# Attention layers of a two-layer transformer block: the order in which one DMA-issuing engine works, and the place of a reciprocal

## Chip, cores and metric

One core of one Trainium2 chip. The metric is device time in microseconds of one execution, lower is better; the kernel's time is the median of three runs.

## What is computed

```python
x = L0_attn_x                                # (8, 512, 256) float32
x = layernorm(x + attn(x))                   # 16 heads of 16, biases, head mask, no causal mask
x = layernorm(x + ffn(x))
# ffn: h = x + causal_attention(rmsnorm(x, g1))          rotary q and k, 16 heads of 16
#      y = h + moe(rmsnorm(h, g2))                       8 experts, top 2 of 8, silu(x wg) * (x wu) @ wd
```

Every attention ends in softmax(scores) @ v. The kernel computes the sum of exponentials (the denominator) beside the weighted sum, so the output of a group of heads has to be divided by its denominators before the output projection.

## The kernel before

The program has three stages: the two attention layers in one stage (`attention_layers`), the routing of tokens to experts, and the expert tiles with the final normalisation. The change lies in the first alone.

**Units, halves, groups.** A unit u is one of the 8 sequences in one of the 2 layers: u 0 to 7 is the first layer ("plain"), 8 to 15 the second ("causal"). A unit has two halves h of 8 heads, a half has two groups of 4 heads; n counts groups from 0 to 63, u is n // 4 and g is n % 4. Every engine runs the same outer loop, one step for each n, and each step has four quarters. In step n TensorE makes the scores of group n (L778, diagonal blocks masked by L839), ScalarE takes their exponentials (L1067), TensorE weighs v with them (L879), and, three groups ahead, TensorE makes the scores from which VectorE takes row maxima (L783, L1171). In between each step does pieces of other units: projections, rotary embedding, the output projection, the residual, statistics.

**The path of a half's output.** ScalarE empties the output of group n - 1 into `a_o` in quarter 2 of step n (L1074). SyncE, which issues every DMA of this stage in one fixed order, stores it in DRAM (`store_o`, L299). When both groups of a half are stored, `load_o` reads back the denominators alone as a 128x32 tile `a_den` (L308) and the outputs without them, `a_o_half` (L312). VectorE inverts `a_den` in place (`invert`, L1259). SyncE stores the inverse (`store_inv`, L317) and reads it back spread over the 16 dimensions of each head, `a_inv_half` (`load_inv`, L325). GpSimd multiplies (`normalise`, L474) and splits the result into high and low halves in float16, `a_aT` (L478, L480). TensorE takes `a_aT` in the output projection (`project_out`, L705), in steps with g = 2, quarters 2 and 3, and VectorE adds the residual (L1301 for the first layer, L1306 for the second).

**What GpSimd does around it.** In an odd step of the second layer GpSimd splits q and k (L455, L460, after VectorE's rotary sum L1271), then calls `normalise`, then in steps with g = 3 adds the residual (L527), then splits a piece of expert weights (L539, L541). In the following even step with g = 2 it makes the low half of the layer's output (`part_low`, L532), for which VectorE's L1306 waits.

**What SyncE does around it.** Its other DMAs are the q and k tiles (L255, L260, L275), the row maxima (`load_rows`, L283, after ScalarE's L1010), the next input (`load_x`, L240 or L245), the residual (`load_res`, L334), stores of results (`store_x`, L343, `store_part`, L352), and in steps 0 to 47 and the one after the pieces of expert weights that are split in the background (`store_weights` L372, `load_weights` L364). A wait on SyncE holds back everything behind it.

The lines that a sentence can't say, of `load_o`:

```python
for i in range(2):
    sync.wait_ge(o_stored[i], 16 * (h + 1))
...
sync.dma_start(den[:, h % 2], heads[:, DH].rearrange("k (c e) -> k c e", e=32)
               ).then_inc(den_loaded[h % 2], 16)
```

## Time and profile before

| | us |
|---|---|
| median of 3 runs | 1419.68 (1417.67 to 1426.33) |
| the profiled execution | 1423.02 |
| its span | 1421.3 |
| TensorE (PE) busy | 1259.9, 89% of the span |
| VectorE (DVE) busy | 959.2, 67% |
| ScalarE (ACT) busy | 823.6, 58% |
| GpSimd (POOL) busy | 778.3, 55% |
| mean granted clock of TensorE | 0.945 of full speed |

The times of one execution are read from its start. The attention stage lasts until about 880 us, the routing until about 930, the expert tiles and the final normalisation to the end. An engine's idle time is put down to what it waited for last.

### The profile page before, as it was taken

Reading aid. Unit: us, or ns where it says so; the run is one execution under the profiler, and the core shown is the slowest. Engines: PE = TensorE matmul, PEld = TensorE weight load, DVE = VectorE, ACT = ScalarE, POOL = GpSimd, SP = SyncE. Lnnn points to the kernel's source line nnn. Section 1 sums busy time; section 2 is a strip of 40 time slices with the busy share of each in tenths; the row PEclk is TensorE's granted clock in tenths of the full one; section 3 lists DMA queues with packets and bytes.
Section 4 is the critical chain, followed back from the end, with each engine's and each line's share of the span. In section 5 each row is a group of like instructions: output and inputs, shape, how many; then the busy total and the mean of one; then the engine's idle time right before and its main releaser. Section 6 shows DMA issues by size and latency. Waiting matters only on the chain. (4 is left out here: it accounts for less than half of the span.)

```text
span 1421.3 us, 33080 instructions
## 1 busy us (share of the span) xinstructions
PE 1259.9 (89%) x11471; PEld 693.0 (49%) x11472; DVE 959.2 (67%) x1776; ACT 823.6 (58%) x1676; POOL 778.3 (55%) x820
## 2 busy tenths in 40 slices
PE   3999999999999999999999995379999999999980
PEld 1222222322223444444444443358888888888860
DVE  7788888888897886978888736924444444444434
ACT  4078788788888776766676663134343434344434
POOL 5044465556546667576645333056666666666643
PEclk7589999999999999999999897689999999999996
DMA  6336676767767878687766433875222222223226
GB/s 183 66 78 175 184 183 188 193 186 204 199 184 215 227 220 226 206 217 200 209 165 164 115 123 126 226 210 121 42 47 42 47 44 45 42 44 48 38 27 240
DMA packets 157657, 202.53 MB, mean 143 GB/s; under 512 B 30760, under 2 KB 120616, under 8 KB 157544
## 3 DMA queue, kind: packets, MB, share of 16 engines
q1 hardware_dynamic: 140968, 181.60, 46.6%
q0 software_dynamic: 16576, 19.45, 8.6%
q8 instruction: 68, 1.11, 0.3%
q14 instruction: 45, 0.37, 0.1%
HBM read 110.40 MB, written 81.81 MB: 135 GB/s over the span
## 5 line engine op out<-in xcount | busy, mean ns | idle before, releaser
L1067 ACT ACTIVATE a_probs<-a_ps_s 128x512 f32<-128x512 f32 (+2 forms) x896 | 460.4, 569 | 165.1 <-PE a_ps_s L778 160.1
L1171 DVE TENSOR_REDUCE a_shift_max<-a_ps_m 128x1 f16<-128x512 f32 x512 | 320.7, 684 | 54.7 <-PE a_ps_m L783 53.4
L783 PE MATMUL a_ps_m<-a_qkx 48*128 48x128 f16 (+3 forms) x1408 | 285.2, 303 | 20.2 <-DVE a_shift_max L1171 8.7
L1868 PE MATMUL e_ps_gu<-e_xT,w_up 128*128 128x256 f16 (+1 forms) x2574 | 290.0, 269 | 4.5 <-issue 3.0
L778 PE MATMUL a_ps_s<-a_qkx 49*128 49x128 f16 (+3 forms) x1408 | 276.0, 296 | 14.3 <-ACT a_probs L1067 14.3
L1868 PEld LDWEIGHTS e_ps_gu<-e_xT,w_up 128*128 x2574 | 242.2, 98 | 38.6 <-issue 8.7
L879 PE MATMUL a_ps_o<-a_probs,a_v_one 128*32 128x512 f32 (+3 forms) x2048 | 233.8, 529 | 2.6 <-ACT a_o L1074 2.6
L778 PEld LDWEIGHTS a_ps_s<-a_qkx 49*128 49x128 f16 x1408 | 90.1, 95 | 265.4 <-ACT a_probs L1067 151.6
L1804 POOL DMA_INDIRECT h<-e_y,e_put x74 | 118.7, 1604 | 88.6 <-DVE e_y L1968 57.6
L474 POOL TENSOR_TENSOR a_o_half<-a_o_half,a_inv_half 128x512 f32<-128x512 f32 x31 | 40.0, 1289 | 222.2 <-DMA a_inv_half<-a_inv_dram 222.2
L1981 DVE TENSOR_TENSOR e_h<-e_gate,e_ps_gu 128x512 f32<-128x512 f32 (+4 forms) x156 | 79.5, 530 | 120.8 <-ACT e_gate L1931 90.2
L1931 ACT ACTIVATE e_gate<-e_ps_gu 128x512 f32<-128x512 f32 (+1 forms) x78 | 44.9, 575 | 196.5 <-PE e_ps_gu L1868 160.6
L1890 PE MATMUL e_ps_y<-w_down,e_h 128*128 x1258 | 146.2, 273 | 11.2 <-issue 9.8
L1171 DVE TENSOR_REDUCE a_neg_off<-a_ps_m 128x1 f32<-128x384 f32 (+2 forms) x256 | 138.6, 545 | 10.6 <-PE a_ps_m L783 9.7
L1988 DVE TENSOR_TENSOR e_h<-e_h 128x512 f16<-128x512 f32 (+4 forms) x156 | 84.3, 540 | 85.2 <-ACT e_h L1936 43.6
L1890 PEld LDWEIGHTS e_ps_y<-w_down,e_h 128*128 128x128 f16 x1258 | 114.7, 97 | 41.3 <-issue 21.4
L455 POOL CAST a_qk<-a_q 128x1024 f16<-128x1024 f32 x32 | 33.2, 1037 | 157.3 <-DVE a_q L1271 91.9
L1171 DVE TENSOR_REDUCE a_neg_max<-a_ps_m 128x4 f32<-128x512 f32 x128 | 87.9, 687 | 42.4 <-PE a_ps_m L783 41.7
L783 PEld LDWEIGHTS a_ps_m<-a_qkx 48*128 48x128 f16 x1408 | 84.7, 95 | 63.2 <-DVE a_shift_max L1171 37.6
L654 PE MATMUL a_ps_x<-a_xT,w_proj 128*128 128x512 f16 x384 | 100.9, 402 | 14.9 <-DVE w_proj L1360 11.0
L1816 POOL DMA_INDIRECT e_share<-weights,e_find x74 | 76.6, 1035 | 42.3 <-issue 42.3
L1790 POOL DMA_INDIRECT e_x<-part,e_take x74 | 74.2, 1003 | 40.5 <-issue 39.1
(240 smaller groups left out, 1673.7 us busy)
## 6 DMA issues: line engine op xcount, KB each, us to landing
a_qkx<-a_qk_dram SPq DMA_DIRECT2D x192, 128.0 KB, 4.3
a_qk_dram<-a_qk SPq DMA_DIRECT2D x32, 512.0 KB
a_o_dram<-a_o SPq DMA_DIRECT2D x62, 256.0 KB, 2.9
part<-a_part SPq DMA_DIRECT2D x16, 512.0 KB, 5.6
a_q_swap<-a_q SPq DMA_DIRECT2D x64, 128.0 KB
a_o_half<-a_o_dram SPq DMA_DIRECT2D x31, 256.0 KB
a_inv_half<-a_inv_dram SPq DMA_DIRECT2D x31, 256.0 KB
spare<-in_wg SPq DMA_DIRECT2D x16, 352.0 KB, 5.6
```

The costliest lines, as they stand in the source:

```text
L654: mm = pe.matmul(ps_x[:], t.w_proj[:, 4 * layer + w, wh, k, m * P:(m + 1) * P], xT[:, u % 2, xh, k, :], start=n == 0, stop=n == 5)
L778: return pe.matmul(out, kx[first:first + 49, r, pair, kt * P:(kt + 1) * P], qx[first:first + 49, r, pair, q0:q1], start=start, stop=stop)
L783: return pe.matmul(out, qx[first:first + 48, r, pair, q * P:(q + 1) * P], kx[first:first + 48, r, pair, k0:k1], start=start, stop=stop)
L879: mm = pe.matmul(ps_o[32 * j:32 * (j + 1), S - w:S], v_one[:, u % 2, kt, g * HG + j, :], probs[:, kt // 2, j, first:first + w], start=kt = ...
L1067: act.activation(dst, src, ACT.Exp).then_inc(exp_out, 1)
L1171: vector.tensor_reduce(out, src, AX.X, ALU.max, negate=True).then_inc(max_out, 1)
L1804: pool.indirect_dma_start(t.h_dram, bass.IndirectOffsetOnAxis(ap=put[:, s, half:half + 1], axis=0), y[:, s, half], None, compute_op=ALU.ad ...
L1816: pool.indirect_dma_start(share[:, s, half:half + 1], None, t.weight_dram, bass.IndirectOffsetOnAxis(ap=find[:, s, half:half + 1], axis=0) ...
L1868: mm = pe.matmul(ps_gu[:, bank, kind, f % 2, 0:width(r, s)], w[:, ds(e, 1)].rearrange("p o f -> p (o f)"), xT[:, s, xh, k, 0:width(r, s)], ...
L1890: mm = pe.matmul(ps_y[:, s, half], h[:, s, hh, f, half * P:(half + 1) * P], w[:, ds(e, 1)].rearrange("p o f -> p (o f)"), start=c == 0, st ...
L1981: op = vector.tensor_tensor(h32[0:rows, bank, m, 0:w], gate[0:rows, bank, m, 0:w], ps_gu[0:rows, bank, 1, m, 0:w], ALU.mult)
L1988: op = vector.tensor_tensor(low, h32[0:rows, bank, m, 0:w], h[0:rows, s, 0, f, 0:w], ALU.subtract)
```

## The change

`after` does the same instructions and the same DMAs with the same waits. Two things stand in another order.

```diff
                 if n % 2 == 0:
                     swap((n + 6) // 2)
                     load_qk((n + 4) // 2)
+                    store_o(n - 1)
+                    load_o(n // 2 - 1)
                     if g == 0:
                         store_part(u - 3)
                         load_res(u - 1)
                     elif u + 3 > 0:
                         load_x(u + 3)
-                    store_o(n - 1)
                     for m in weights_at(n - 1):
                         store_weights(m)
                         load_weights(m + 2)
-                    load_o(n // 2 - 1)
                 else:
+                    store_inv((n - 3) // 2)
                     load_rows((n + 1) // 2)
+                    load_inv((n - 3) // 2)
                     load_last(n - 1)
                     load_last(n)
-                    store_inv((n - 3) // 2)
                     store_o(n - 1)
                     if g == 3:
                         store_x(u - 2)
-                    load_inv((n - 3) // 2)
...
                         if quarter < 2:
                             rope_sum((n + 5) // 2, quarter)
-                        if quarter == 1:
+                        if quarter == 0:
                             invert((n - 3) // 2)
```

SyncE, steps 40 and 41 (second layer, h = 19). `a_o` is a group's output, `part` and `a_x_res` the layer's result and the residual, `w_down` and `spare` the expert weights. Before:

```order
L352 DMA part<-a_part 128x4x512
L334 DMA a_x_res<-x 128x4x256
L299 DMA a_o_dram<-a_o 128x512
L372 DMA w_down_hi<-a_w_part 128x704
L372 DMA w_down_lo<-a_w_part 128x704
L364 DMA spare<-in_wd 128x704
L308 DMA a_den<-a_o_dram 128x1x32
L312 DMA a_o_half<-a_o_dram 128x1x512
L283 DMA a_qkx<-a_rows 1x4x512 x2
L317 DMA a_inv_dram<-a_den 128x32
L299 DMA a_o_dram<-a_o 128x512
L325 DMA a_inv_half<-a_inv_dram 128x1x512
```

The same place of SyncE in the changed kernel:

```order
L299 DMA a_o_dram<-a_o 128x512
L308 DMA a_den<-a_o_dram 128x1x32
L312 DMA a_o_half<-a_o_dram 128x1x512
L352 DMA part<-a_part 128x4x512
L334 DMA a_x_res<-x 128x4x256
L372 DMA w_down_hi<-a_w_part 128x704
L372 DMA w_down_lo<-a_w_part 128x704
L364 DMA spare<-in_wd 128x704
L317 DMA a_inv_dram<-a_den 128x32
L283 DMA a_qkx<-a_rows 1x4x512 x2
L325 DMA a_inv_half<-a_inv_dram 128x1x512
L299 DMA a_o_dram<-a_o 128x512
```

The store of the output and the two loads that wait for it moved ahead of the result, the residual and the three weight DMAs; the store of the inverse moved ahead of the rows, and its load ahead of the next store of an output.

VectorE in step 41, before. `a_neg_off` and `a_neg_max` are row maxima of a later group, `a_q` the rotary sum:

```order
L1271 TENSOR_TENSOR a_q<-a_q_cos,a_q_swap 128x512
L1171 TENSOR_REDUCE a_neg_off<-a_ps_m 128x2
L1171 TENSOR_REDUCE a_neg_max<-a_ps_m 128x2x2
L1171 TENSOR_REDUCE a_neg_off<-a_ps_m 128x1
L1326 SCALAR_TENSOR_TENSOR a_hid<-a_hid,a_rms,g 128x256
L1271 TENSOR_TENSOR a_q<-a_q_cos,a_q_swap 128x512
L1259 RECIPROCAL a_den<-a_den 128x32
```

and in the changed kernel:

```order
L1271 TENSOR_TENSOR a_q<-a_q_cos,a_q_swap 128x512
L1259 RECIPROCAL a_den<-a_den 128x32
L1171 TENSOR_REDUCE a_neg_off<-a_ps_m 128x2
L1171 TENSOR_REDUCE a_neg_max<-a_ps_m 128x2x2
L1171 TENSOR_REDUCE a_neg_off<-a_ps_m 128x1
L1326 SCALAR_TENSOR_TENSOR a_hid<-a_hid,a_rms,g 128x256
L1271 TENSOR_TENSOR a_q<-a_q_cos,a_q_swap 128x512
```

The reciprocal moved ahead of one quarter's three maxima, one scaling and the second rotary sum.

## Rows read from the trace of the kernel before

**Rows 1.** Windows: time, busy us by engine (instructions), granted clock, DMA share, GB/s.

```profile
303.53:354.12 50.59, 47.50 (x339) 14.50 (x337) 44.68 (x81) 42.79 (x85) 28.71 (x30) 1.00 0.72 194
509.30:556.35 47.05, 44.59 (x512) 19.99 (x511) 39.56 (x76) 33.17 (x70) 29.78 (x30) 1.00 0.80 225
556.35:607.80 51.45, 47.48 (x514) 20.96 (x515) 43.38 (x72) 32.87 (x74) 32.73 (x27) 0.93 0.76 218
607.80:658.03 50.23, 46.60 (x557) 21.67 (x556) 40.49 (x70) 32.80 (x72) 33.83 (x27) 1.00 0.81 218
658.03:707.87 49.84, 47.10 (x550) 21.47 (x547) 39.06 (x69) 32.70 (x73) 29.88 (x24) 0.97 0.72 192
707.87:755.31 47.44, 46.02 (x555) 21.57 (x556) 39.46 (x71) 32.70 (x72) 26.46 (x20) 1.00 0.70 176
...
802.49:855.71 53.22, 49.61 (x570) 22.43 (x567) 23.38 (x46) 35.67 (x83) 12.10 (x11) 0.96 0.37 111
```

**Rows 2.** Waits of GpSimd and VectorE: us in total, times, longest us.

```profile
POOL a_o_half L474 <- DMA a_inv_half<-a_inv_dram: 222.2, 31, 20.9
...
DVE a_hid L1306 <- POOL a_part L532: 15.7, 4, 6.5
...
DVE a_den L1259 <- DMA a_den<-a_o_dram: 1.5, 2, 0.9
```

**Rows 3.** Timeline around 600 us, VectorE and GpSimd: start us, us, instruction, idle before.

```profile
593.32 2.01 DVE L1271 TENSOR_TENSOR a_q<-a_q_cos,a_q_swap 128x512 f32<-128x512 f32 x1
...
597.90 0.34 DVE L1259 RECIPROCAL a_den<-a_den 128x32 f32<-128x32 f32 x1
...
599.16 2.13 POOL L460 TENSOR_TENSOR a_qk<-a_q,a_qk 128x1024 f16<-128x1024 f32 x1
603.95 1.27 POOL L474 TENSOR_TENSOR a_o_half<-a_o_half,a_inv_half 128x512 f32<-128x512 f32 x1 [2.66 <-DMA a_inv_half<-a_inv_dram]
...
612.48 0.69 DVE L1306 TENSOR_TENSOR a_hid<-a_ps_x,a_x_res 128x512 f32<-128x512 f32 x1 [4.11 <-POOL a_part L532]
```

**Rows 4.** Timeline of TensorE at 558 us.

```profile
557.93 2.71 PE L705 MATMUL a_ps_x<-w_proj,a_aT 128*128 128x256 f16 x12 [2.53 <-POOL a_aT L480]
```

**Rows 5.** Timeline of SyncE around the same inversion: its DMA issues.

```profile
586.17 0.38 SPq L352 DMA_DIRECT2D part<-a_part  x1
586.65 0.45 SPq L334 DMA_DIRECT2D a_x_res<-x  x1
587.15 1.04 SPq L299 DMA_DIRECT2D a_o_dram<-a_o  x1
...
589.68 0.43 SPq L364 DMA_DIRECT2D spare<-in_wd  x1
593.58 0.65 SPq L308 DMA_DIRECT2D a_den<-a_o_dram  x1
594.28 0.63 SPq L312 DMA_DIRECT2D a_o_half<-a_o_dram  x1
594.96 1.29 SPq L283 DMA_DIRECT2D a_qkx<-a_rows  x2
598.27 0.32 SPq L317 DMA_DIRECT2D a_inv_dram<-a_den  x1
...
599.68 0.64 SPq L325 DMA_DIRECT2D a_inv_half<-a_inv_dram  x1
```

**Rows 6.** Windows in that stretch, same columns as the first group.

```profile
589.50:592.50 3.00, 2.87 (x36) 0.93 (x29) 2.94 (x6) 2.02 (x5) 3.00 (x4) 1.00 1.08 375
```

**Rows 7.** DMA issues 598 to 601 us: KB each, median us to landing.

```profile
a_inv_dram<-a_den SPq DMA_DIRECT2D x1, 16.0 KB, 1.4
```

**Rows 8.** Timeline of SyncE and GpSimd near the end of the stage.

```profile
825.36 0.33 SPq L299 DMA_DIRECT2D a_o_dram<-a_o  x1
...
827.40 0.62 SPq L308 DMA_DIRECT2D a_den<-a_o_dram  x1
...
832.20 1.28 SPq L283 DMA_DIRECT2D a_qkx<-a_rows  x2
...
835.06 0.64 SPq L325 DMA_DIRECT2D a_inv_half<-a_inv_dram  x1
839.01 1.27 POOL L474 TENSOR_TENSOR a_o_half<-a_o_half,a_inv_half 128x512 f32<-128x512 f32 x1 [8.97 <-DMA a_inv_half<-a_inv_dram]
```

## The prediction

> **What bounds the kernel now.** I read the busy shares by engine first, then the table of waits, then windows of one unit each, and last the timeline at the places where the windows are too long. TensorE is busy for 89% of the span, but the change touches only the attention stage, and only its waits, so the question is which wait there ends last. The table of waits has a large candidate: GpSimd idles 222.2 us in 31 pieces for the inverse that comes back from DRAM [rows 2]. That is no gain in itself, since GpSimd is not the engine that sets the pace. What counts is who waits behind it.
>
> In the first layer nobody does. A unit there takes 50.59 us with TensorE 47.5, VectorE 44.7 and ScalarE 42.8 busy, and GpSimd 28.7 [rows 1]: GpSimd's idle time is cover. In the second layer a unit that starts at the normalisation before its output projection takes 47.05 us where nothing stalls, but the next three take 51.45, 50.23 and 49.84, and then one takes 47.44 [rows 1]. At the start of the first long one TensorE waits 2.53 us for `a_aT`, and its 12 matmuls then take 2.71 us [rows 4]; the window has a granted clock of 0.93 [rows 1]. At the start of the second VectorE waits 4.11 us for GpSimd's `part_low` [rows 3], one of four such waits of 15.7 us, the longest 6.5 [rows 2]. GpSimd reaches `part_low` late because `normalise` ahead of it sat 2.66 us for the inverse [rows 3]. So the second layer has a chain: store of the output, denominators back, reciprocal, store of the inverse, inverse back, `normalise`, `part_low`, residual. It ends last once in a unit, and this is the chain that the change shortens.
>
> **The change, step by step, for the half inverted at 597.9 us.** *Denominators.* Before, the output store is issued at 587.15 and the denominators, which wait for it, at 593.58: 6.43 us [rows 5]. The same pair with nothing ahead takes 2.04 us (825.36 to 827.40) [rows 8]. The gain is therefore at most 4.4 us plus the 0.98 us of issue ahead of the store (586.17 to 587.15), and at least that 0.98. Ahead of the store stand the q and k loads, which stay there, and two transfers of 512 KB, which go behind. At the rate of the stretch, 375 GB/s [rows 6], these two take 1.05 MB / 375 = 2.8 us, nearer to the bytes than to either end. I take the denominators 2.7 us sooner: issued at 590.9.
>
> *Behind them.* SyncE still has to issue the output's load, the result, the residual and three weight DMAs. Before, the stretch from 586.17 to the end of the last weight issue at 590.11 plus the output's load of 0.63 comes to 4.57, less the output's store of 1.04: 3.5 us. SyncE is free at 590.9 + 0.65 + 3.5 = 595.0.
>
> *Reciprocal.* It now follows the first rotary sum, which ends at 593.32 + 2.01 = 595.3, and takes 0.34 [rows 3]: done at 595.7 and not 598.2. The denominators have to be there by 595.3; the nearest small transfer, 16 KB, lands in 1.4 us [rows 7], so they are there at 592.3, and the cover is 3.0 us. Even at their old time (593.58 + 1.4 = 595.0) VectorE would not wait. The maxima behind the reciprocal start 0.34 us later and those behind its old place as before: nothing.
>
> *Store and load of the inverse.* SyncE issues the store at 595.8. Here the new order has its price: the output's load, result, residual and weights, 1984 KB or 2.03 MB that before had mostly drained, have been issued in the 4 us ahead of it. At 375 GB/s [rows 6] they need 5.4 us from 591.0, to 596.4, and the store lands at 595.8 + 1.4 = 597.2 as if alone. In the meantime SyncE issues the rows for 1.29 us [rows 5], to 597.4, so the inverse's load goes out at 597.4 and not at 599.68: 2.3 us. The load itself took 603.95 - 599.68 = 4.27 us [rows 3, 5] behind an output store and takes 3.95 at the quietest place [rows 8], so another 0.2 comes from that. The inverse arrives 2.5 us sooner. GpSimd sat idle 2.66 us there, from the end of its split of q and k at 601.29 [rows 3], so almost all of it is used; the next to end last is that split.
>
> The rate decides this step. 375 GB/s is a stretch with large transfers alone; over a whole unit, with the small descriptors of q and k in it, the rate is 218 to 225 [rows 1]. At 218 the 2.03 MB last 9.3 us, to 600.3, and the inverse's store, if it has to let them pass, would land at some 601.2 and its load go out 1.5 us later than now. I take 375, since what stands in this backlog is what ran at that rate, and keep the other end for a rival.
>
> That a small store pays for what was issued ahead of it is the rule of the Trainium skill that speaks against this change. The page "DMA: Bandwidth & Descriptors" says, in "Queues, rings and completion order", that each DMA engine takes descriptors in ring order and that a semaphore's increment lands only after every earlier write of that engine. Without the rule the store would land in 1.4 us at any rate, each stall would give 2.5 us whatever the backlog, and the rival below would fall away. The output store bears the rule out: 6.43 us behind other transfers against 2.04 alone [rows 5, 8].
>
> **The sum.** I apply 2.5 us to each unit's stall.
>
> - Unit at 556: TensorE's wait of 2.53 us goes, and the excess over a unit without a stall is 51.45 - 47.05 = 4.4 us, of which the rest is half-speed matmuls behind the wait (the clock of 0.93). I take 3.9, since the clock may fall for another reason.
> - Unit at 608: 2.5 of 4.11 us of wait, on an excess of 3.18: 1.9.
> - Unit at 658: the four waits of VectorE sum to 15.7, less 6.5 and 4.11 leaves 5.1 for two, this being the larger with some 3.3. 2.5 of 3.3, on an excess of 2.79: 2.1.
> - Unit at 708: excess 0.39, all of it: 0.4.
> - End of the stage (unit at 802, VectorE's wait of 6.5 us): no weights are moved there, and the output store has nothing ahead, so the denominators gain nothing. The inverse's load follows the rows, issued at 832.20 for 1.28 us, at 833.5 and not at 835.06 [rows 8]: 1.5 us sooner.
> - First layer: the same sooner inverse shortens GpSimd's idle time and nobody's wait: 0. The transfers that now start 3 to 4 us later (next input, residual, result, weight pieces) are needed a step, 12 us, later or more; at nothing, with that step as cover. If the residual came late, GpSimd's idle time for the inverse would still stand behind it.
>
> Together 3.9 + 1.9 + 2.1 + 0.4 + 1.5 = 9.8 us. The profiled execution took 1423.02 us (span 1421.3), 3.3 above the median of 1419.68; against its own time the sum gives 1413.2, and carried to the median 1409.9. I say **1410 us**.
>
> **Rivals.** *The backlog cancels it* (no change). The inverse's load goes out when it did before if the backlog ends at about 598.7, 7.7 us from 591.0, a rate of 264 GB/s; that is between the two rates above. For it: the unit's mean is under that. Against: the stretch itself was at 375, and halves in steps with g = 2 have 512 KB less ahead. Then only the 1.5 us at the end, where no weights are moved, are left: 1418.
>
> *More than the stalls goes* (faster). GpSimd idles a few us before each normalisation of the second layer; with these gone, q and k are stored sooner too and no stretch falls to half clock. All four excesses (10.8 us) and the 6.5 us at the end: 17.3 us, 1402.
>
> *The backlog delays the inverse* (slower). The same mechanism beyond that point: weights, result and residual are issued as one block directly ahead of the inverse's store, and at 218 GB/s they hold it until 601.2. The inverse is then 1.5 us later than before at each of the eight normalisations of the second layer that stand ahead of an output projection, the unit without a stall included: 8 x 1.5 = 12 us, 1432. It decides from 264 GB/s down. The rows of maxima, issued right behind the store, would be late with it and could only add to this.
>
> *The change doesn't do what it says*: excluded by the listed order, which has the moves on both engines.
>
> **Chances.** Forecast (5 to 14 us faster) 0.52; no change (within 5 either way) 0.24; more than 14 faster 0.14; slower by more than 5, 0.10. Some 1%, 14 us, is what a measurement of this kernel can tell from no change. So faster by over 1% 0.15, within 1% 0.77 (part of the slower case lies within), slower by over 1% 0.08. The range takes in the forecast, the case without gain, and the nearer part of the faster one: 1401 to 1422.
>
> **What the changed profile should show.** GpSimd's idle time for the inverse well below 222 us, near 130; 31 halves with an output store and denominators 3 to 5 us apart; VectorE's reciprocal directly after the first rotary sum with at most 2 us of waiting in all; the wait of VectorE for `part_low` down from 15.7 to some 7 us; units of the second layer at 47 to 48.5 us; units of the first layer unchanged at 50.6. I am wrong if VectorE's wait at L1259 is over 10 us, if the inverse's store takes over 4 us to land, or if the first layer's units change.

## The result and the profile after

The changed kernel takes 1466.46 us (median of 4 runs, 1465.73 to 1468.12), the kernel before 1418.68 in the same comparison (1417.25 to 1426.33): 1.033 times as long, with a 95% interval from 1.031 to 1.035. That is 47.8 us more, where 9.8 less were forecast.

The busy times, from the page of the changed kernel's profile:

```profile
span 1464.2 us, 33080 instructions
PE 1285.2 (88%) x11471; PEld 699.3 (48%) x11472; DVE 963.0 (66%) x1776; ACT 827.1 (56%) x1676; POOL 774.8 (53%) x820
```

VectorE, ScalarE and GpSimd are as busy as before, within 4 us. TensorE is busy for 25 us more with the same instructions: its mean granted clock was 0.936, after 0.945. The waits of the whole run (us in total, times, longest us), against [rows 2]:

```profile
POOL a_o_half L474 <- DMA a_inv_half<-a_inv_dram: 207.5, 31, 17.4
...
PEld a_ps_m L783 <- DMA a_qkx<-a_qk_dram: 33.9, 16, 5.7
...
POOL a_x_res L489 <- DMA a_x_res<-in_x: 31.0, 6, 8.6
...
PE a_ps_m L783 <- DMA a_qkx<-a_qk_dram: 29.5, 16, 5.5
```

GpSimd's idle time for the inverse, which I wanted at 130 us, only fell from 222.2 to 207.5. Two waits stand out that were small or absent before: TensorE waits for the q and k tiles of the maxima (in the attention stage, from 100 to 900 us, 3.1 us before and 27.0 now), and GpSimd for the residual, 31.0 us, all in the first layer. TensorE's wait for `a_aT`, which the forecast set out to remove at one place, hardly moved: 5.9 us before, 5.3 now. VectorE's wait for the denominators is gone, and its wait for `part_low` is down from 15.7 to 3.3 us; so two of the signs that I named came true while the time went the other way. Of the three signs of being wrong, two came: the inverse's store took over 4 us to land, and the first layer's units changed.

The engine that was moved says more. The waits of SyncE, the changed kernel:

```profile
SPq L307 <- DMA a_o_dram<-a_o: 133.3, 29, 6.3
SPq L275 <- DMA a_qk_dram<-a_qk: 84.7, 31, 5.9
SPq L325 <- DMA a_inv_dram<-a_den: 82.7, 29, 4.8
SPq L283 <- ACT a_rows L1010: 62.0, 20, 22.9
SPq L317 <- DVE a_den L1259: 20.4, 12, 5.7
```

and of the kernel before:

```profile
SPq L307 <- DMA a_o_dram<-a_o: 120.0, 29, 6.8
SPq L283 <- ACT a_rows L1010: 114.9, 26, 24.7
SPq L275 <- DMA a_qk_dram<-a_qk: 85.7, 31, 7.4
...
SPq L325 <- DMA a_inv_dram<-a_den: 15.3, 18, 2.1
```

SyncE stands 67.4 us longer for the inverse to land in DRAM and 13.3 us longer for the output. What went down is its wait for ScalarE (L283), 52.9 us: time in which SyncE was ahead of the engines. That was its slack, and the change spent it.

Windows of four units of the second layer as one, then of seven units of the first (columns as in [rows 1]). Before:

```profile
499.28:695.91 196.63, 183.69 (x2101) 83.11 (x2101) 158.66 (x279) 132.13 (x287) 129.53 (x106) 0.97 0.78 217
139.56:499.28 359.72, 340.01 (x2532) 109.32 (x2529) 311.24 (x559) 297.22 (x583) 207.63 (x204) 1.00 0.72 195
```

and after:

```profile
518.67:737.32 218.65, 197.60 (x2106) 86.67 (x2105) 156.90 (x280) 134.47 (x288) 129.05 (x106) 0.90 0.73 195
138.04:518.67 380.63, 347.32 (x2524) 109.99 (x2522) 315.57 (x560) 298.41 (x582) 209.83 (x205) 0.98 0.70 184
```

Here a unit runs from ScalarE's emptying of the output of its first group (L1074) to the next unit's. The second layer's four units lost 22.0 us: 13.9 in which TensorE was busy longer (the clock fell from 0.97 to 0.90) and 8.1 in which it stood idle. The first layer's seven lost 20.9: 7.3 busy and 13.6 idle. The DMA engines have the same bytes to move and are busy for a smaller share, 0.73 after 0.78. Over a whole unit the loss is not a lack of bandwidth; DMAs are issued later. In the last units, which have no weights to move, the time is 137.4 before and 138.8 after.

The same half as in [rows 3, 5, 7] (h = 19), SyncE in the changed kernel:

```profile
618.74 0.42 SPq L299 DMA_DIRECT2D a_o_dram<-a_o  x1
624.10 0.65 SPq L308 DMA_DIRECT2D a_den<-a_o_dram  x1
...
628.42 0.49 SPq L364 DMA_DIRECT2D spare<-in_wd  x1
628.95 0.51 SPq L317 DMA_DIRECT2D a_inv_dram<-a_den  x1
629.50 1.29 SPq L283 DMA_DIRECT2D a_qkx<-a_rows  x2
635.64 0.63 SPq L325 DMA_DIRECT2D a_inv_half<-a_inv_dram  x1
...
638.28 0.74 SPq L260 DMA_DIRECT2D a_qk_dram<-a_qk  x1
639.12 3.52 SPq L255 DMA_DIRECT2D a_q_swap<-a_q  x4
643.72 2.85 SPq L275 DMA_DIRECT2D a_qkx<-a_qk_dram  x6
646.61 0.42 SPq L299 DMA_DIRECT2D a_o_dram<-a_o  x1
```

Read two gaps. From the output's store to the denominators SyncE stands still for 4.9 us with nothing behind it issued. From the rows to the inverse's load it stands again, 4.85 us (630.79 to 635.64): the store of 16 KB took 6.7 us to land. Before, the first pair was 6.43 us apart, but with three weight DMAs issued in between [rows 5], and the second landing took 1.4 us [rows 7]. Over the stretch from 500 to 800 us the median time of the inverse's store from issue to landing went from 1.4 us to

```profile
a_inv_dram<-a_den SPq DMA_DIRECT2D x11, 16.0 KB, 5.0
```

GpSimd ended the split of q and k at 635.27, and its store goes out at 638.28. One even output store to the next is 27.9 us (618.74 to 646.61); before it was 23.5 (587.15 to 610.66). SyncE's own round is longer by 4.4 us. Some 0.5 of that is that the result and the residual fall into this round now and the next input into the other; the rest is its two waits.

Why the store was late is seen in the landing times of one block, from 512.4 to 523 us of the changed kernel (KB each, median us from issue to landing):

```profile
part<-a_part SPq DMA_DIRECT2D x1, 512.0 KB, 5.6
a_x_res<-in_x SPq DMA_DIRECT2D x1, 512.0 KB, 7.4
spare<-in_wd SPq DMA_DIRECT2D x1, 352.0 KB, 6.7
...
a_inv_dram<-a_den SPq DMA_DIRECT2D x1, 16.0 KB, 6.3
```

and in the windows of that stretch:

```profile
511.00:513.00 2.00, 1.95 (x17) 0.81 (x17) 0.69 (x1) 0.49 (x1) 1.30 (x1) 0.55 0.01 2
513.00:516.00 3.00, 3.00 (x23) 1.06 (x21) 2.56 (x5) 2.64 (x6) 0.00 (x0) 0.50 0.62 133
516.00:519.00 3.00, 3.00 (x29) 1.18 (x26) 2.02 (x4) 2.48 (x6) 0.20 (x1) 0.50 1.03 340
```

While SyncE waits for the output to land the DMA engines run dry (share 0.01, 2 GB/s); then the block of 1984 KB (output's load, result, residual, weights) starts from nothing, and the small store behind it lands with it. The Trainium skill says on the page "DMA: Bandwidth & Descriptors", in "Queues, rings and completion order", that a semaphore's increment lands only after every earlier write of the same DMA engine; it is the rule that the prediction weighed. The trace agrees: the last piece of the block, issued at 516.12, landed 6.7 us later, at 522.8, and the store, issued at 516.64, 6.3 us later, at 522.9.

How SyncE's lateness reaches the q and k tiles is seen one half earlier, where h = 18 is inverted, in the changed kernel:

```profile
605.56 0.63 SPq L325 DMA_DIRECT2D a_inv_half<-a_inv_dram  x1
...
610.39 0.46 SPq L260 DMA_DIRECT2D a_qk_dram<-a_qk  x1
...
616.03 2.66 SPq L275 DMA_DIRECT2D a_qkx<-a_qk_dram  x6
```

GpSimd's split of q and k had ended at 605.05. SyncE stood until 605.56 for the inverse, then had five issues to make up, and stored q and k only at 610.39, 5.3 us after they were ready; before the change, at the same place, it was 1.0 us (split ended at 576.55, store at 577.51). The loads that depend on that store go out at 616.03, and TensorE's timeline shows the wait for such loads:

```profile
511.05 0.50 PE L783 MATMUL a_ps_m<-a_qkx 48*128 48x256 f16 x2 [2.28 <-DMA a_qkx<-a_qk_dram]
...
623.77 0.60 PE L783 MATMUL a_ps_m<-a_qkx 48*128 48x256 f16 x2 [5.47 <-DMA a_qkx<-a_qk_dram]
```

with windows around the second:

```profile
610.00:616.00 6.00, 6.00 (x76) 3.44 (x75) 5.43 (x10) 3.77 (x8) 5.86 (x5) 1.00 1.01 328
616.00:620.00 4.00, 2.31 (x26) 0.77 (x24) 1.35 (x3) 1.69 (x3) 3.84 (x5) 1.00 0.82 142
620.00:624.00 4.00, 0.23 (x2) 0.16 (x3) 0.00 (x0) 0.00 (x0) 3.92 (x4) 0.55 0.81 131
624.00:626.00 2.00, 2.00 (x17) 0.70 (x15) 0.81 (x2) 0.64 (x2) 0.18 (x1) 0.50 0.05 8
```

TensorE stands for 5.47 us and afterwards works at 0.50 of full speed, its 1.2 GHz level. So a wait is followed by a second price, longer matmuls.

### The profile page after: what moved, and what is told of

It reads as the page before. It is cut to its first block and busy times, and to the rows that moved or that the text cites. A ratio compares the mean times of both kernels' runs of the same rounds, so it can differ in the third digit from the quotient of the medians.

```text
span 1464.2 us, 33080 instructions
## 1 busy us (share of the span) xinstructions
PE 1285.2 (88%) x11471; PEld 699.3 (48%) x11472; DVE 963.0 (66%) x1776; ACT 827.1 (56%) x1676; POOL 774.8 (53%) x820
## 5 line engine op out<-in xcount | busy, mean ns | idle before, releaser
L1067 ACT ACTIVATE a_probs<-a_ps_s 128x512 f32<-128x512 f32 (+2 forms) x896 | 462.4, 569 | 204.0 <-PE a_ps_s L778 198.9
L783 PE MATMUL a_ps_m<-a_qkx 48*128 48x128 f16 (+3 forms) x1408 | 291.9, 309 | 44.4 <-DMA a_qkx<-a_qk_dram 29.5
L778 PE MATMUL a_ps_s<-a_qkx 49*128 49x128 f16 (+3 forms) x1408 | 284.9, 304 | 13.5 <-ACT a_probs L1067 13.0
L879 PE MATMUL a_ps_o<-a_probs,a_v_one 128*32 128x512 f32 (+3 forms) x2048 | 237.5, 537 | 2.6 <-ACT a_o L1074 2.6
L1171 DVE TENSOR_REDUCE a_neg_off<-a_ps_m 128x1 f32<-128x384 f32 (+2 forms) x256 | 138.7, 545 | 26.8 <-PE a_ps_m L783 26.0
L474 POOL TENSOR_TENSOR a_o_half<-a_o_half,a_inv_half 128x512 f32<-128x512 f32 x31 | 39.5, 1274 | 207.5 <-DMA a_inv_half<-a_inv_dram 207.5
L654 PE MATMUL a_ps_x<-a_xT,w_proj 128*128 128x512 f16 x384 | 108.0, 423 | 13.6 <-DVE w_proj L1360 10.9
L1816 POOL DMA_INDIRECT e_share<-weights,e_find x74 | 76.0, 1027 | 42.3 <-issue 42.3
L1790 POOL DMA_INDIRECT e_x<-part,e_take x74 | 72.0, 973 | 40.2 <-issue 40.2
```

Source lines behind the costliest of these rows:

```text
L654: mm = pe.matmul(ps_x[:], t.w_proj[:, 4 * layer + w, wh, k, m * P:(m + 1) * P], xT[:, u % 2, xh, k, :], start=n == 0, stop=n == 5)
L778: return pe.matmul(out, kx[first:first + 49, r, pair, kt * P:(kt + 1) * P], qx[first:first + 49, r, pair, q0:q1], start=start, stop=stop)
L783: return pe.matmul(out, qx[first:first + 48, r, pair, q * P:(q + 1) * P], kx[first:first + 48, r, pair, k0:k1], start=start, stop=stop)
L879: mm = pe.matmul(ps_o[32 * j:32 * (j + 1), S - w:S], v_one[:, u % 2, kt, g * HG + j, :], probs[:, kt // 2, j, first:first + w], start=kt = ...
L1067: act.activation(dst, src, ACT.Exp).then_inc(exp_out, 1)
L1171: vector.tensor_reduce(out, src, AX.X, ALU.max, negate=True).then_inc(max_out, 1)
```

## The experiments

The theory after the result: SyncE is near its limit, and time in which it stands still for a landing is the loss. The rivals: it is the backlog's delay of the inverse alone (the rival of the prediction, larger than priced); or VectorE or GpSimd wait at a new place. The experiments first take the change apart, then move single pieces. "Before" as baseline of a diff is the kernel before, "changed" the kernel after. Differences in us are taken from 1418.68 and 1466.46, the medians above. The ratios are each run's own comparison with the kernel before, which had 1416.95 to 1418.89 there; so a difference in us is good to some 2 us.

**The half of the change in even steps.** From before:

```diff
                     load_qk((n + 4) // 2)
+                    store_o(n - 1)
+                    load_o(n // 2 - 1)
...
-                    store_o(n - 1)
...
-                    load_o(n // 2 - 1)
```

> Only the even steps are changed: store of the output, denominators and output load ahead of result or input, residual and weight pieces; odd steps and VectorE as before. Theory 1 (the block of 1.5 to 2 MB now stands directly ahead of the inverse's store, which lands 5 us after its issue instead of 1.7, and SyncE stands still meanwhile, so the q and k tiles come late): most of the loss is here, 1440 to 1465 us, and SyncE's wait at L325 is 50 us or more, not 15. Theory 2 (the reciprocal ahead of the row maxima holds VectorE): nothing or a gain here, 1410 to 1420.

Measured: 1440.09 us, 1.016 times before (1.012 to 1.020). Nearly half of the loss comes from this alone. SyncE's wait for the inverse's landing rises from 15.3 to 46.7 us although its store and load stand where they stood: the block of transfers now starts late and is in front of them. The waits of TensorE say what that costs: for `a_aT` 20.0 us in the attention stage, after 5.9, and for q and k only 4.7. That is the late inverse of the prediction's slower rival, by itself.

**The half in odd steps, with the reciprocal.** From before:

```diff
+                    store_inv((n - 3) // 2)
                     load_rows((n + 1) // 2)
+                    load_inv((n - 3) // 2)
...
-                    store_inv((n - 3) // 2)
...
-                    load_inv((n - 3) // 2)
...
-                        if quarter == 1:
+                        if quarter == 0:
```

> Only the odd steps and VectorE are changed: store of the inverse ahead of the rows, its load right behind them, reciprocal a quarter sooner; even steps as before. Theory 1: no block ahead of the inverse's store, so no loss, 1408 to 1421 us, with SyncE's wait at L325 under 25 us and GpSimd's wait for the inverse under 200. Theory 2: the whole loss, 1450 to 1470, with VectorE waiting over 10 us at L1259.

Measured: 1432.49 us, 1.013 (1.009 to 1.016). VectorE waits 16.1 us for the denominators and SyncE 61.8 us for the reciprocal. The two halves alone lose 21.4 and 13.8 us, together 35.2 of 47.8; what is left only appears when both are there.

**The reciprocal alone.** From before:

```diff
-                        if quarter == 1:
+                        if quarter == 0:
```

> Only the reciprocal moves, a quarter sooner on VectorE; SyncE's order is as before. Theory 1: 1415 to 1421 us, no difference. Theory 2: the denominators, which come as late as before, hold up the maxima: 1435 or more.

Measured: 1436.6 us, 1.013 (1.009 to 1.017). The waits of VectorE:

```profile
DVE a_den L1259 <- DMA a_den<-a_o_dram: 19.5, 15, 2.7
```

The loss of 17.9 us is nearly all in the first layer (374.6 us for its seven units after 359.7), while the second layer's four units are even 2.2 us shorter (194.4). The waits are not: 9.6 of the 19.5 us fall before 500 us, 9.9 after. So a wait of VectorE costs in the first layer, where it is next to the pace, with 44.7 of 50.59 us busy [rows 1]. The reciprocal early in the second layer alone was not tried. In the changed kernel this wait is nought, since the denominators come earlier.

**The change without the reciprocal's move.** From changed:

```diff
-                        if quarter == 0:
+                        if quarter == 1:
```

> The whole change of SyncE's order, the reciprocal as before. Since VectorE waits 0.0 us for denominators in the changed kernel, Theory 1 (SyncE's two uncovered waits in a cycle of two steps) gives no less than the change itself, 1460 to 1480 us: the inverse's store now waits for a later reciprocal and the rows stand behind it. If the quarter is part of the loss in combination too, under 1455.

Measured: 1474.6 us, 1.041 (1.038 to 1.043). Inside the full change the reciprocal's move is a gain of 8.1 us (1.041 against 1.033); VectorE is not where the loss lies.

**The inverse's load back at its place.** From changed:

```diff
                     load_rows((n + 1) // 2)
-                    load_inv((n - 3) // 2)
...
                         store_x(u - 2)
+                    load_inv((n - 3) // 2)
```

> The whole change, but the load of the inverse stands again behind the next output store and the store of x. Theory 1: the two issues ahead of the wait hide only 0.5 to 1 us of 5, so it stays slow, 1450 to 1466 us. Theory 1b (the block alone is harmless, it is the early load of the inverse that holds the output store and all behind it): most of the loss goes, under 1430.

Measured: 1433.16 us, 1.012 (1.008 to 1.015). One line gives back 33.3 of 47.8 us. SyncE's wait at that load falls from 82.7 to 37.3 us, as other issues lie between the store and its load again, TensorE's for the q and k tiles from 27.0 to 2.1, and the first layer is back at 361.0 us. This is the largest single step. GpSimd still waits 13.8 us for the residual here, so a wait of that size costs the first layer next to nothing. In the second layer's four units 9.1 us of the loss stay, with 14.9 us of TensorE's waiting for `a_aT`: the late inverse again.

**The inverse's load alone moved forward.** From before:

```diff
                     load_rows((n + 1) // 2)
+                    store_inv((n - 3) // 2)
+                    load_inv((n - 3) // 2)
...
-                    store_inv((n - 3) // 2)
...
-                    load_inv((n - 3) // 2)
```

> Only the load of the inverse moves, ahead of the output's store in odd steps; the bulk transfers and VectorE stay. Theory 1': with nothing large ahead of the inverse's store it lands in 1.5 us and the uncovered wait is small: 1415 to 1424 us, TensorE's wait for q and k under 6 us. If the early load costs by itself whatever is ahead, 1430 or more.

Measured: 1436.33 us, 1.012 (1.009 to 1.015), with 40.6 us of SyncE's waiting for the inverse to land and 12.4 us of TensorE's for q and k. The inverse's store, which moves with it, lands as before here (1.77 us from the store to its load over 31 halves, 1.70 before). The early load costs 17.7 us even without the block behind an idle stretch.

**Only the output's store ahead.** From before:

```diff
                     load_qk((n + 4) // 2)
+                    store_o(n - 1)
...
-                    store_o(n - 1)
```

> Only one thing is moved in the kernel before: in even steps the output's store goes ahead of result, residual or input; the loads that wait for it stay behind the weight pieces, and odd steps and VectorE are as before. Theory A (every load that waits for its store is harmless as long as the bulk transfers stand between them, the loss is SyncE standing still with idle DMA engines): the denominators are issued 2 us sooner, SyncE's wait at L307 falls, and the time is 1410 to 1420 us. Theory B (result, residual and input must go out first, whatever SyncE waits for): 1425 or more, with GpSimd waiting for the residual at L489.

Measured: 1412.87 us, 0.997 (0.995 to 0.999): a gain of 0.3%, small but clear of none by its interval. The waits of SyncE:

```profile
SPq L283 <- ACT a_rows L1010: 161.2, 32, 24.6
SPq L275 <- DMA a_qk_dram<-a_qk: 82.1, 30, 6.4
SPq L307 <- DMA a_o_dram<-a_o: 66.3, 29, 4.5
```

Here the store is followed by its old neighbours, which are issued while it lands, and the wait for it halves from 120.0 to 66.3 us. The time saved appears as slack for ScalarE's rows, 161.2 after 114.9. It is the one part of the change that moves a DMA forward without a wait for a landing moving with it, and the best version here. Where the gain arises is not settled: in the profiled executions the seven and the four units are within 1 us of before, and the last three units, without weights, take 131.8 us after 137.4.

**The same, with the inverse's store and the reciprocal early.** From the kernel of the last experiment:

```diff
+                    store_inv((n - 3) // 2)
                     load_rows((n + 1) // 2)
...
-                    store_inv((n - 3) // 2)
...
-                        if quarter == 1:
+                        if quarter == 0:
```

> As the run before, and the reciprocal a quarter sooner with the inverse's store ahead of the rows; the inverse's load stays where it was. If VectorE's 19.5 us at L1259 came only from denominators 2 us too late, they fall under 5 us and the time is 1405 to 1418. If they stay over 10 us, 1425 to 1435.

Measured: 1423.79 us, 1.005 (1.003 to 1.007). VectorE waits 11.9 us for denominators that left only 1 to 2 us sooner, and SyncE 114.1 us at the inverse's store. Here too the first layer loses (371.0 us) and the second layer's four units gain (192.9, the least of all versions).

**The same as the best, the inverse's load ahead of the result.** From that kernel:

```diff
+                    load_inv((n - 3) // 2)
                     if g == 3:
                         store_x(u - 2)
-                    load_inv((n - 3) // 2)
```

> The output's store ahead of result, residual or input in even steps, and in odd steps the load of the inverse ahead of the store of x (512 KB), behind the output's store. Theory 1': the inverse lands about 1 us sooner in steps with g = 3 and nothing else moves: 1409 to 1415 us against 1413 of the store alone. A loss of over 5 us would say that even 0.5 us of uncovered wait counts.

Measured: 1421.64 us, 1.002 (1.000 to 1.005), from 12 runs of 1413.63 to 1430.48. One DMA of cover less, and the gain is gone; TensorE's wait for q and k is 8.2 us.

**Weights of even steps issued in the odd ones.** From changed:

```diff
-                    for m in weights_at(n - 1):
-                        store_weights(m)
-                        load_weights(m + 2)
                 else:
...
-                    for m in weights_at(n - 1):
+                    for m in weights_at(n - 2) + weights_at(n - 1):
```

> The whole change, but the weight pieces of even steps (704 KB) are issued in the odd step behind the load of the inverse and the stores, with that step's own. Theory 1 (the inverse's store lands late behind the block, and SyncE waits for it at L325): that wait falls from 83 us by at least a third, TensorE's wait for q and k tiles with it, and the time is 1430 to 1450. Theory C (the length of SyncE's order is what counts, not the bytes ahead of the inverse): L325 stays over 65 us and the time at 1460 or more.

Measured: 1472.01 us, 1.040 (1.035 to 1.044). With 704 KB less ahead of it SyncE's wait for the inverse's landing fell from 82.7 to 48.7 us, so the backlog does decide the landing. But the kernel got no faster: 45.4 us are now spent waiting for the reciprocal at the inverse's store. If the inverse's delay by the backlog were the whole loss, this would have helped. What the landing gives back is taken at the wait next in line, since the two stand in one issuer. The run has a weakness: the late weights now stand ahead of the store of q and k, and GpSimd's wait for the swapped q rises from 7.1 to 17.1 us, so it does not separate the two theories cleanly.

**q and k stored ahead of the inverse's load.** From changed:

```diff
-                    load_inv((n - 3) // 2)
...
                     store_o(n - 1)
+                    store_qk((n + 5) // 2)
+                    load_inv((n - 3) // 2)
...
-                    store_qk((n + 5) // 2)
```

> The whole change, but in odd steps the output's store and the store of q and k go out ahead of the load of the inverse and its wait. Theory 1' (of the change's 48 us the larger part, some 30, is the wait for the landed inverse standing ahead of the store of q and k, whose load TensorE needs at the start of the second step after): TensorE's wait for q and k tiles falls from 27 us to under 8 and the time to 1425 to 1442, although SyncE still stands still at L325. Theory C (SyncE's total of waits is what counts): over 1455.

Measured: 1459.09 us, 1.029 (1.026 to 1.032). The first layer is back at 360.9 us and the second is as bad as before, 219.8 for its four units. There the store of q and k waits for GpSimd's split (42.3 us at L260 over the run, 5.5 in the changed kernel), and the inverse waits behind it: TensorE now stands 16.7 us for `a_aT`. I had expected both layers to recover. The first layer's loss is the issue of q and k and its surroundings held up by the inverse; the second layer's is not that alone. The last three units lose here too, 149.8 us after 137.4.

**The same store early in the best version.** From that kernel:

```diff
                     store_o(n - 1)
+                    store_qk((n + 5) // 2)
                     if g == 3:
...
-                    store_qk((n + 5) // 2)
```

> The output's store ahead of result, residual or input in even steps, and in odd steps the store of q and k directly behind the output's store, ahead of the store of x, the load of the inverse and the weight pieces. Theory 1': q and k tiles come sooner, where they were late TensorE gains, but the inverse's load waits for GpSimd's split of q and k: between 1405 and 1420 us. Clearly slower, over 1425, if the inverse is the tighter of the two.

Measured: 1479.67 us, 1.044 (1.042 to 1.047). A clear miss, and the slowest kernel of all: SyncE waits for GpSimd at L260 and at the weights' store (34.0 and 23.2 us), the inverse's load stands behind that, and GpSimd, which has to normalise before it splits weights, waits for the inverse. It is again a wait put ahead of work that others need.

**The inverse's load issued by GpSimd.** From changed:

```diff
-                    load_inv((n - 3) // 2)
...
             def normalise(h):
...
+                    pool.wait_ge(inv_stored[s], 16 * (h // 2 + 1))
...
+                    pool.dma_start(inv_half[:, s], src.broadcast_to([8, DH, S])).then_inc(inv_loaded[s], 16)
```

> The whole change, but the load of the inverse is issued by GpSimd, which waits for it anyway, directly ahead of normalise; SyncE no longer waits at L325. All bytes and their order of need stay. Theory S (SyncE standing still is the loss): 83 us of its waits go, and the time falls from 1466 to 1410 to 1435. Theory T (traffic: the inverse lands late behind the bulk transfers whoever issues it): 1455 or more.

Measured: 1475.78 us, 1.042 (1.036 to 1.047). Half of what it was to show came: TensorE's wait for q and k fell from 27.0 to 5.8 us once SyncE no longer waited for the inverse's landing. But GpSimd asks for the inverse only after its own split and then waits for all of it (lines are shifted by 4):

```profile
POOL a_o_half L478 <- DMA a_inv_half<-a_inv_dram: 160.8, 30, 8.3
POOL a_inv_half L475 <- DMA a_inv_dram<-a_den: 76.6, 12, 13.3
PE a_ps_x L709 <- POOL a_aT L484: 33.4, 11, 4.1
```

The hand-over adds a wait of TensorE of its own, 33.4 us after 5.3 in the changed kernel, so that the total says nothing of how much SyncE's wait was worth.

**The same hand-over in the best version.** From that kernel, the same lines.

> The output's store ahead of result, residual or input in even steps as in e5, and the inverse's load issued by GpSimd. Theory S: SyncE waits only 12 us there in e5, so little is to be had: 1405 to 1418. If GpSimd's own issue is dear, 1420 or more.

Measured: 1471.85 us, 1.040 (1.036 to 1.044), 59 us slower than the version that it is made from. SyncE has 194.8 us of slack at L283 and TensorE waits 41.0 us for `a_aT`. Slack on the issuer is worth nothing if the engine that issues instead is on the path.

**The second layer without its weight traffic, changed and before.** The pieces of `w_down` (numbers 32 to 47, counted from 0, all moved in the second layer) are neither loaded nor stored in the stage, so that its content is left out; GpSimd's splits stay, and the stores are made behind the stage. From changed and from before:

```diff
-                if 0 <= m < NW:
+                if 0 <= m < NW and m < KEPT:
```

> The whole change without the loads and stores of the 16 weight pieces of the last matrix during the second layer (left out of the computation: w_down's content; GpSimd still does the splitting, and 32 stores follow at the end of the stage). To be read against e16. Theory S and Theory T both: the 29 us of the second layer shrink, under 10, since SyncE gets 48 issues (some 25 us) of slack back and the DMA engines 704 KB a step less. Were the loss in VectorE's or GpSimd's order, all 29 would stay.

> The kernel before with the same left out (w_down's content), as the measure for e15: 1415 to 1440 us with the stores at the end; the difference of the two is what the change costs with slack given back: 15 us of the first layer, and 0 to 10 of the second.

Measured: 1451.17 us, 1.024 (1.021 to 1.027), and 1421.98, 1.005 (1.003 to 1.006). The changed order is 29.2 us behind, not 47.8. Windows of the same four units of the second layer, the changed order and the order before:

```profile
517.88:714.03 196.15, 183.94 (x2101) 83.65 (x2101) 159.83 (x279) 132.33 (x287) 129.13 (x106) 0.97 0.67 169
```

```profile
496.56:685.07 188.51, 181.94 (x2101) 82.28 (x2101) 158.89 (x279) 131.95 (x288) 129.86 (x106) 0.98 0.68 169
```

A loss of 7.6 us where it was 22.0, and the clock stays at 0.97. Two thirds of the second layer's loss hang on the weight traffic; of the first layer's, where nothing was taken away, 16.2 us stay (and 22.0 in the next pair; so a sum of one profiled execution varies).

**Only the bytes taken away.** The same DMAs are issued, with 32 of 704 columns each (of `w_down` again only that much is moved in the stage, and its content is left out). From changed and from before:

```diff
-                        sync.dma_start(dst, w_part[:, m % 2, hl]).then_inc(w_stored[m % 2], 16)
+                        sync.dma_start(dst[:, 0:cut(m)], w_part[:, m % 2, hl, 0:cut(m)]).then_inc(w_stored[m % 2], 16)
```

> The whole change; the weight DMAs of the last 16 pieces are all issued, but each moves 32 of 704 columns (left out of the computation: w_down's content; 32 full stores follow at the end of the stage). To be read against e18, units 8 to 11. Theory S (SyncE's own time: issues and the waits for landings): the issues are back but the landings of the inverse and output are quicker for lack of bytes, so the loss is above e15's 8 us, 12 to 20, if issue time counts. Theory T (bytes): about 8 us or less, as in e15 against e16.

> The kernel before with the same small weight DMAs (w_down's content left out), the measure for e17: 1418 to 1428 us, as e16; units 8 to 11 at 187 to 192 us.

Measured: 1461.47 us, 1.031 (1.027 to 1.034), and 1425.54, 1.006 (1.004 to 1.008). The four units take 199.4 and 189.2 us:

```profile
519.11:718.47 199.36, 185.08 (x2101) 83.48 (x2101) 153.99 (x279) 132.90 (x287) 128.52 (x106) 0.97 0.68 167
```

```profile
495.63:684.88 189.25, 181.69 (x2101) 82.86 (x2101) 158.81 (x280) 131.71 (x288) 129.99 (x106) 0.98 0.69 171
```

So the loss of 22.0 us is 10.1 with the issues and their waits kept and the bytes gone, and 7.6 with both gone. The 10.1 lies between what the two theories had asked for, nearer to the one in which the bytes count. The split is some 12 us for the bytes of the weights, 2.5 for their issue, and 7.6 for the order of what remains. The first layer, the same in both pairs, came out 5.8 us apart, so the 12 is a size and the 2.5 is not told from nothing. That the bytes act by way of the late landing and of the clock is read from the traces: TensorE's wait for q and k is 11.3 us here and 8.5 with no weight DMAs, after 27.0, and the clock is 0.97.

Side by side (us). The units are those above; "chain" is SyncE's waiting in the chain that was moved: for the output to land (L304, L307), for the reciprocal (L317) and for the inverse to land (L325), over the run.

| kernel | median | first layer, 7 units | second, 4 units | chain |
|---|---|---|---|---|
| output's store alone | 1412.87 | 358.8 | 196.3 | 98.7 |
| before | 1418.68 | 359.7 | 196.6 | 155.2 |
| best with inverse's load ahead | 1421.64 | 361.1 | 198.0 | 97.2 |
| best with inverse's store and reciprocal early | 1423.79 | 371.0 | 192.9 | 165.3 |
| odd steps and reciprocal | 1432.49 | 366.7 | 198.1 | 195.2 |
| changed, inverse's load back | 1433.16 | 361.0 | 205.7 | 201.1 |
| inverse's load alone | 1436.33 | 364.7 | 208.8 | 187.5 |
| even steps alone | 1440.09 | 365.0 | 207.7 | 198.9 |
| changed | 1466.46 | 380.6 | 218.7 | 243.0 |
| changed, weights late | 1472.01 | 381.6 | 221.9 | 234.8 |
| changed, reciprocal late | 1474.60 | 381.9 | 218.8 | 270.7 |

The kernels stand almost in the order of that last column, up to some 150 us at little cost and then steeply. Out of the row fall those in which the order adds a wait elsewhere: the reciprocal alone (138.3, with VectorE's 19.5 us), the two with q and k stored early (192.0 and 97.5, with SyncE's waits for GpSimd), and the two hand-overs to GpSimd (212.5 and 73.0, with TensorE's waits for `a_aT`). So the column orders the kernels; it does not prove that the waiting is the cause.

SyncE's waits in the four units of the second layer, for landings and for engines: 42.6 and 20.6 us before, 74.4 and 5.5 in the changed kernel, 26.8 and 38.1 with the output's store alone. The 20.6 us are all that was to spare in 196.6, and the change asked for 31.8 more. In the seven units of the first layer they are 120.7 and 40.2 before and 157.9 and 14.3 after.

## Why the prediction was wrong

Point by point, by its own steps.

- *"I take the denominators 2.7 us sooner."* Half right: at h = 19 the pair is 5.36 us apart (618.74 to 624.10), not 6.43, and over all 31 halves the mean went from 6.14 to 5.17. The gain is at the low end of the bracket that I gave. Transfers of q and k stand ahead of the store in both orders; that it waits for them is the likely reason, not a tested one.
- *Reciprocal, cover 3.0 us.* Right: VectorE's wait at L1259 is nought in the stage after the change, and without that move the changed kernel is 8.1 us slower. The cover came from the sooner denominators: alone the move costs 17.9 us. So the sentence "Even at their old time ... VectorE would not wait" was wrong: it was read from one half, and with the denominators at their old time (the reciprocal alone) VectorE waited 19.5 us, in 15 pieces.
- ***"... the store lands at 595.8 + 1.4 = 597.2 as if alone."*** This step failed, and it carried the forecast. I let the backlog drain at 375 GB/s from 591.0. At h = 19 the store landed 6.7 us after its issue, and over 31 halves the time from the store to its load went from 1.70 to 5.03 us. The rate was read in a stretch in which the engines were already full. In the new order they are empty when the block begins, since SyncE has issued nothing while it waited: 133 GB/s in the first 3 us, then 340. Of the 1984 KB issued from 512.44 us on the bulk was moved at about 521.3, which is 229 GB/s, and the last landing came at 522.8, which is 196. I had 218 as the other end, and its rival at a chance of 0.10, while the mean of a unit, the only rate in the rows that includes the start, spoke for it. It decides from 264 down. Yet the landing is not the whole of it: with the store landing as fast as before, the early load alone cost 17.7 us.
- *The price of that rival*, 12 us, was for the inverse alone. With the even steps alone, where that mechanism shows by itself, 21.4 us were measured; for the whole change it was too small by a factor of four, because it took no account of what SyncE's standing still holds back.
- ***"First layer: ... nobody's wait: 0"*, and 12 us of cover for the moved transfers.** This step failed as well: 20.9 us in seven units. I asked of each moved transfer whether its data were needed soon. I did not ask what SyncE as an engine can do in a unit. Each of the two waits moved ahead of everything else holds back all of it, in the first layer too, and the cover of 12 us for the residual was used up: GpSimd waited 31.0 us for it, up to 8.6 at once. Whether that wait cost anything is not shown; with 13.8 us of it the first layer was at 361.0.
- *The sum over stalls*: 3.9 + 1.9 + 2.1 + 0.4 + 1.5. VectorE's stall went where it stood (for `part_low`, 15.7 to 3.3 us), TensorE's for `a_aT` did not (5.9 to 5.3), and the four units from L1074 to L1074, 47.1, 49.0, 50.2 and 50.3 us before, became 57.1, 55.7, 56.9 and 49.1, since TensorE's wait for q and k took its place, with half clock behind it. I had excluded no such wait; I had not looked for one.

What the runs show: the inverse's load put early is the largest part (33.3 us when put back, 17.7 when moved alone), by SyncE's standing still; the output's load put early, right behind its store, is the second part (21.4 us alone, and a gain of 0.3% when only the store moves); the bytes of the weights in the block add to it (some 12 us of the second layer's 22.0). What stays open: how the rest of the second layer's loss divides between the time that SyncE needs to issue and the loop in which late q and k make late outputs. The two hand-overs to GpSimd were to settle it and brought a wait of their own. That the clock's fall follows from TensorE's waits is how the rows lie in time (5.47 us of waiting, then 0.50), and was not tested by itself.

## What to carry to other kernels

An engine that issues DMAs in one order is a resource like the others. Before a wait is moved forward on it, add up its waits for engines, which are its slack (here 20.6 of 197 us), and its waits for landings, and leave between a store and the load that waits for it the bulk of the issues that need nothing. Move the store forward without its load: that alone gained 0.3% here, where store and load together lost 1.6%. To price a small transfer behind a block, ask whether the DMA engines are full or empty when the block starts.

## What was not expected of the hardware

A 16 KB store issued at the end of a block of 1984 KB that started on idle DMA engines landed 6.3 to 6.7 us after its issue, where it took 1.4 us before [rows 7]; the first 3 us of the block ran at 133 GB/s. The inverse's load, which took 4.27 us when SyncE issued it [rows 3, 5] and 4.3 in the changed kernel (median over the 30 halves in which GpSimd waited for it, from issue to normalisation), took longer from GpSimd's queue, in the hand-over from the changed kernel (500 to 800 us, KB and median us to landing):

```profile
a_inv_half<-a_inv_dram POOLq DMA_DIRECT2D x11, 256.0 KB, 7.0
```

A stand of TensorE of 2.3 us (at 509 us) was followed by half clock for some 10 us, although TensorE was busy again: the granted clock was 0.55 from 511 to 513 us, 0.50 from 513 to 521 and 0.93 from 521 to 524. After the stand of 5.47 us it was 0.50 from 624 to 632 and 0.65 from 632 to 635.
